# State-space layer and FP4 feed-forward on one core: x kept in place, written-out start lists, 54 unread fp32 products

## What is computed

```python
def _L0_attn_ref(x, A, B, C, D, gamma, beta):
    xB = jnp.einsum('bsh,nh->bsn', x, B)
    xD = jnp.einsum('bsh,oh->bso', x, D)
    def step(state, xb_t):
        state = state @ A.T + xb_t
        return (state, state)
    ...
    out = jnp.einsum('bsn,hn->bsh', states, C) + xD
    ...
    return (out - mu) * rsqrt(var + LN_EPS) * gamma + beta

def _L0_ffn_ref(x, w_gate, w_up, w_down):      # 256 -> 704 -> 256
    gate = fp4_linear(x, w_gate)               # both operands rounded to FP4,
    y = fp4_linear(x, w_up)                    # one scale for 16 elements
    h = jax.nn.silu(gate) * y
    return fp4_linear(h, w_down)

x = _layernorm(x + _L0_attn_ref(x, ...))
x = _layernorm(x + _L0_ffn_ref(x, ...))
```

## Time and profile before

| | us |
|---|---|
| median of 3 runs | 607.63 |
| the profiled run | 608.48 |
| its span | 606.7 |
| outside its span | 1.78 |
| first x load issued | 1.75 |
| first product of tile 0 (`layer`) | 75.86 |
| `gu0` of tile 0 | 96.93 |
| `gu0` of tile 3 | 124.74 |
| span end | 606.7 |

### The profile page before, as it was taken

The page is one execution under the profiler, slowest core; times in us unless marked ns, Lnnn a source line. Parts: engine busy times, 40 slices in busy tenths (PEclk is TensorE's granted clock), DMA queues, the critical chain, the costliest instruction groups (busy, mean ns, idle before and its releaser), DMA issues.

```text
span 606.7 us, 12733 instructions
## 1 busy us (share of the span) xinstructions
PE 566.4 (93%) x3699; PEld 504.2 (83%) x3699; DVE 511.2 (84%) x1226; ACT 473.2 (78%) x1424; POOL 494.2 (81%) x672
## 2 busy tenths in 40 slices
PE   7986577899999999999999999999999999999974
PEld 6763555799999999999999999999999999999864
DVE  4484124699999999999999999999999999999971
ACT  2663255578888888888888888888888888888763
POOL 3243163789999999999999999999999999998642
PEclk9997676899999999999999999999999999999997
DMA  6653031111112111111111111111111111100001
GB/s 214 261 202 102 2 84 39 33 38 39 56 56 58 55 57 57 56 55 55 55 55 55 55 55 55 55 55 55 55 55 55 55 55 55 55 26 18 18 21 41
DMA packets 46268, 38.35 MB, mean 63 GB/s; under 512 B 7008, under 2 KB 44960, under 8 KB 45216
## 3 DMA queue, kind: packets, MB, share of 16 engines
q1 hardware_dynamic: 46240, 38.00, 20.6%
HBM read 19.50 MB, written 8.39 MB: 46 GB/s over the span
## 4 chain that ended last, share of the span: by engine, by line
PE 85%; DVE 6%; ACT 3%; DMA 2%; issue 2%; SPq 1%; POOL 1%; POOLq 0%; DVEq 0%; ACTq 0%
PE gu L1089 39%; PE turned L1089 18%; PE yb L1089 7%; PE turned L1143 7%; DMA scratch<-in_L_attn_x_dram 2%; PE turned L1110 2%; PE yb L978 1%; PE yb L1100 1%; PE gu L978 1%; PE turned L1154 1%; PE turned L1153 1%; PE grid L919 1%; DVE scratch L858 1%; DVE htLo L887 1%; PE gu L1011 1%
## 5 line engine op out<-in xcount | busy, mean ns | idle before, releaser
L1089 PE MATMUL gu<-wguHi,xtHi 128*128 128x512 f32 (+1 forms) x384 | 152.7, 398 | 0.4 <-DVE xtLo L851 0.2
L1089 PE MATMUL gu<-wguLo,xtHi 128*128 128x512 f32 (+1 forms) x384 | 145.2, 378 | 0.0
L1089 PE MATMUL gu<-wguHi,xtLo 128*128 128x512 f32 (+1 forms) x384 | 145.2, 378 | 0.0
L1089 PE MATMUL turned<-wdHi,htHi 128*128 128x256 f32 x320 | 92.3, 289 | 3.8 <-DVE htLo L887 3.8
L499 POOL TENSOR_TENSOR scratch<-scratch 128x704 f32<-128x704 f32 x64 | 92.2, 1441 | 2.5 <-DVE scratch L872 1.8
L1089 PE MATMUL turned<-wdHi,htLo 128*128 128x256 f32 x320 | 91.8, 287 | 0.0
L1089 PE MATMUL turned<-wdLo,htHi 128*128 128x256 f32 x320 | 90.9, 284 | 0.0
L504 POOL TENSOR_TENSOR scratch<-scratch 128x640 f32<-128x640 f32 x64 | 81.9, 1279 | 9.6 <-DVE scratch L882 9.6
L1089 PEld LDWEIGHTS gu<-wguHi,xtLo 128*128 128x128 f32 x384 | 73.1, 190 | 12.6
L1089 PEld LDWEIGHTS gu<-wguHi,xtHi 128*128 128x128 f32 x384 | 73.3, 191 | 10.3 <-DVE xtLo L851 1.0
L1089 PEld LDWEIGHTS gu<-wguLo,xtHi 128*128 128x128 f32 x384 | 73.3, 191 | 8.7
(11 more groups left out here) (191 smaller groups left out, 1650.8 us busy)
## 6 DMA issues: line engine op xcount, KB each, us to landing
scratch<-in_L_attn_x_dram SPq DMA_DIRECT2D x8, 1024.0 KB, 5.0
xtTile<-xT SPq DMA_DIRECT2D x64, 128.0 KB, 2.3
scratch<-in_L_attn_x_dram SPq DMA_DIRECT2D x64, 128.0 KB, 2.4
out_dram<-scratch SPq DMA_DIRECT2D x64, 128.0 KB, 1.9
stTile<-statesHi SPq DMA_DIRECT2D x128, 8.0 KB, 1.8
stTile<-statesLo SPq DMA_DIRECT2D x64, 8.0 KB, 1.7
scratch<-in_L_ffn_w_down_dram SPq DMA_DIRECT2D x1, 704.0 KB, 6.2
scratch<-in_L_ffn_w_up_dram SPq DMA_DIRECT2D x1, 640.0 KB, 6.0
```

Of the source, the lines that this page charges most:

```text
L1089: ins = nc.tensor.matmul(to, l, r, start=(first and q == 0), stop=(last and q == len(passes) - 1))
```

## The change

1. **x in place.** `xRaw` goes. x is loaded into `xT` itself, transposed from there and copied back to the same place (`x_columns`), so no load waits. `xT` is laid out by half, token, and then columns; `load_columns` reads 256 columns of a partition in one piece. The transposes of the second half use `grid` in place of `yb`, and the weights' transposes have two banks in place of three.
2. **Buffers.** The tiles' buffers lie over parts of `scratch` that are used up earlier, or in free room; the output of `mean_square` that nobody reads goes to `yb` and not to `junk`.
3. **Lists.** The preamble and the first six to eight steps of the tiles (VectorE 6, TensorE 7, ScalarE and GpSimd 8) are written out call by call on ScalarE, VectorE, TensorE and GpSimd; the tables are gone. From then on `run` is as before. Two copies of the x groups (0 and 28) go to VectorE. SyncE issues all loads of x and weights without a wait between them, then the small ones.
4. **Silu table.** ScalarE's first instruction is a Silu of one column that nobody reads.
5. **Unread products.** The transposes of `busy` become fp32 products, 10 of them at the start. The 42 others go; in their place `unread_up` adds 54 fp32 products of the identity: 6 before the first `layer`, 24 from there to `gu0` of tile 0, and 4 ahead of each `gu0` of tiles 1 to 6.

The loop, the last steps and all arithmetic that is read are as before. Of the diff:

```diff
-        xTile = view(RING * H).rearrange("p (b k) -> p b k", b=RING)
...
+        xTile = view(FREE, RING * H, RING)
...
             def load_x(h):
-                if h >= 2:
-                    sp.wait_ge(s_xt, 4 * (h - 1))
-                sp.dma_start(xRaw[:, h % 2, :], x_v[h].rearrange("p t d -> p (t d)")).then_inc(s_xload[h % 2], 16)
...
+                sp.dma_start(xT[:, h, :, :, :].rearrange("p t c k -> p (t c k)"),
+                             x_v[h].rearrange("p t d -> p (t d)")).then_inc(s_xload[h], 16)
...
-            load_x(4)
+            for h in range(4, HALVES):
+                load_x(h)
...
-            sp.wait_ge(s_xtc, 4)
+            copied(sp, 3)
             for tile in range(RING):
                 load_columns(0, tile)
+            for tile in range(RING):
+                sp.dma_start(xTile[:, tile, :], x_v[0, :, tile, :]).then_inc(s_ldx[tile], 16)
+            sp.wait_ge(s_sthi, 1)
+            load_states(0, 0, (0, 1))
             sp.wait_ge(s_states, 1)
-            load_states(0, 0)
-            sp.wait_ge(s_xt, 4 * HALVES)
-            sp.wait_ge(s_wlo, len(W_GROUPS))
+            load_states(0, 0, (2,))
...
+            act.wait_ge(s_half, 1)
+            nc.scalar.activation(unread[:, :], neg_half[:, :], ACT.Silu)
...
             def busy(n):
                 for _ in range(n):
-                    nc.tensor.transpose(wbanks[1][:, 0:P], ident[:, :], ident[:, :])
-
-            busy(12)
+                    nc.tensor.matmul(wbanks[1][:, 0:P], ident[:, :], ident[:, :], start=True, stop=True)
+
+            def unread_up(n):
+
+                for _ in range(n):
+                    nc.tensor.matmul(gu[:, 0:P], ident[:, :], ident[:, :], start=True, stop=True)
...
+                    if not isinstance(tile, int) or tile >= 1:
+                        pe.wait_ge([s_silu, s_h, s_hsc][k], done(h, m - 1))
+                        if k == 0 and isinstance(tile, int) and tile <= 6:
+                            unread_up(4)
```

More of the change, by code:

```diff
@@ L264, in ssm_fp4_ffn, with copied, run @@
         PEELED = 2
-        def run(eng, ops, after={}):
+        def copied(eng, u):
+            eng.wait_ge(s_xtc, sum(k not in VECTOR_COPIES for k in range(u + 1)))
+            if min(VECTOR_COPIES) <= u:
+                eng.wait_ge(s_xtcv, sum(k in VECTOR_COPIES for k in range(u + 1)))
+        def run(eng, ops, first):
             last = max(lag for _, lag in ops)
@@ new lines, in _ @@
+            ve1(0, 4)
+            norm2(0, 3)
+            t_hi(0, 6)
+            silu_gate(0, 1)
+            nm2(0, 4)
+            h_abs(0, 0)
+            x_abs(0, 3)
+            sq2(0, 4)
+            ve2(0, 4)
+            states_hi(1)
+            x_hi(0, 2)
+            nr2(0, 4)
+            norm2(0, 4)
+            mean_square(0, 5)
+            t_hi(0, 7)
+            ve1(0, 5)
+            h_hi(0, 0)
+            nm2(0, 5)
+            h_abs(0, 1)
+            silu_gate(0, 2)
+            x_abs(0, 4)
@@ new lines, in _ @@
+            link(0, 1)
+            w_recip(5)
+            link(0, 2)
+            w_lo(2)
+            link(0, 3)
+            w_lo(3)
+            link(0, 4)
+            w_lo(4)
+            link(0, 5)
+            w_lo(5)
+            link(0, 6)
+            w_sum(4)
+            w_sum(5)
+            link(0, 7)
+            w_grid(4)
+            w_grid(5)
+            states_lo(0)
+            xt_copy(28)
+            w_lo(6)
+            w_lo(7)
+            w_lo(8)
+            w_lo(9)
@@ L1095, in layer @@
                 tile = h * CHUNK + m
+                if isinstance(tile, int) and tile == 0:
+                    copied(pe, 15)
+                    pe.wait_ge(s_cstack, 48)
                 pe.wait_ge(s_tlo, done(h, m))
@@ L1155, in ffn_down @@
                                  stop=True).then_inc(s_dn, 1)
-            def fill_links(h, m):
-                tile = h * CHUNK + m
-                if isinstance(tile, int):
-                    if tile == 1:
-                        chunk_states(1)
-                    for k in FILL_CHAIN.get(tile, ()):
-                        link(1, k)
-            gu0, gu1, gu2 = (ffn_up(k) for k in range(3))
-            run(pe, [(h_turn, 6), (gu1, 4), (gu2, 4), (x_turn, 3), (layer, 0), (fill_links, 0), (ffn_down, 6), (gu0, 3)],
-                {0: [lambda: pair_sums(BATCH - 1)]})
+            gu0, gu1, gu2 = (ffn_up(k) for k in range(3))
@@ new lines, in _ @@
+            unread_up(4)
+            layer(0, 1)
+            chunk_states(1)
+            unread_up(4)
+            link(1, 0)
+            layer(0, 2)
+            link(1, 1)
+            unread_up(3)
+            link(1, 2)
+            unread_up(4)
+            link(1, 3)
+            unread_up(4)
+            x_turn(0, 0)
+            unread_up(3)
+            layer(0, 3)
+            gu0(0, 0)
+            link(1, 4)
+            gu1(0, 0)
+            x_turn(0, 1)
+            gu2(0, 0)
@@ new lines, in _ @@
+            link(1, 5)
+            layer(0, 4)
+            gu0(0, 1)
+            link(1, 6)
+            gu1(0, 1)
+            link(1, 7)
+            gu2(0, 1)
+            link(1, 8)
+            x_turn(0, 2)
+            layer(0, 5)
+            gu0(0, 2)
+            h_turn(0, 0)
+            gu1(0, 2)
+            layer(0, 6)
+            gu2(0, 2)
+            x_turn(0, 3)
+            ffn_down(0, 0)
+            gu0(0, 3)
+            run(pe, [(h_turn, 6), (gu1, 4), (gu2, 4), (x_turn, 3), (layer, 0), (ffn_down, 6), (gu0, 3)], FILLED["pe"])
```

712 lines of the change are left out of this document (491 added, 221 removed).

## The result

The changed kernel takes **604.33 us** (median of 11 runs, 603.05 to 606.44) against 607.63 of the kernel before in the same series; the ratio is 0.9947, 95% interval 0.993 to 0.9964. It is faster, by 3.3 us. The forecast was 592.7 with a range of 580 to 602: the direction was right, the size was not, and the time lies outside the range. The profiled run took 604.36 us, its span is 602.6; forecast was a span of 591.8. So 10.8 us have to be found.

A forecast was written before the change was run, and what follows sets the result against it. A long even part bounded by TensorE behind an uneven start; the start of `gu0` of tile 3 decides. Span 606.7 - 17.9 + 3.0 = 591.8, plus 1.8 outside it 593.6, less the profiled run's 0.9: 592.7 us, range 580 to 602.

The forecast's parts named there:

- The fill's own work: First `layer` to `gu0` of tile 3: TensorE's own work at full clock 39.3 us, 40 with uncovered waits.
- Steps (d) to (f): End of pair 1's sums at 44.5 us to first `layer` at 66.8: states, links, x and weight groups, sums of pair 2.
- With a start at about 2 us the columns land at about 31 us: Start: 11.2 MB ahead of tile 0's columns take 28.8 us at 390 GB/s; stall of some 11 us.
- The upper bound of 16: Stall at tile 0's columns: at most 16 us, if SyncE is held and issues twelve small loads late.
- Step (b): After the columns land: TensorE's nine x and weight groups, 8.1 us at half clock, and two powers, 0.5; ends at 41.0.
- step (c): After (b): `pair_sums(1)` taken at half clock, 3.5 us, ending at 44.5.
- 0.7 of uncovered waits: First `layer` to `gu0` of tile 3: TensorE waits only 0.7 us beyond its own 39.3 us of work.
- rival 2: Fill: clock stays down, half-clock TensorE work adds 17.4 us, giving 610.1; chance 0.06.
- (1) No stall: Start: tile 0's columns land by 20 us, ScalarE goes on 11 us earlier, giving 582.7; chance 0.14.
- (3) Half clock up to the first `layer`: Before the first `layer`: 14 groups of (d) and (e) at 0.9 us, 5.3 more, giving 598.0; chance 0.13.
- (4): Even part: a VectorE or GpSimd step longer by 0.3 us lifts 57 steps, giving 598.4; chance 0.04.
- (5): Start: written lists fit better, waits and half clock in (b) and (c) vanish, 6 us less, 586.7; chance 0.15.

The follow-up runs named there:

- e5_x67_last: Changed kernel with x loads of halves 6 and 7, gamma and beta issued behind the small loads and columns of tiles 0 to 3; 597.48 us.
- g1_all_waits: Changed kernel with late column splits, `tMat` loads ahead of the last four x loads, x of tiles 4 to 7 early, all 54 unread products; 577.27 us.
- e1_beta4: Changed kernel with GpSimd's `add_beta` of tile 4 moved behind `pow2` of tile 0, `t_lo` of tile 3 and `pow1` of tile 1; 601.94 us.
- f1_x_early: Changed kernel with x loads of tiles 4 to 7 issued on SyncE before the first states are waited for; 597.65 us.

## Why the prediction was wrong where it was, step by step

**Right.** A stall at the split of the first columns, with every engine behind it (16.89 us at the named instruction). The product at 0.25 us (0.22), the 12 late ones at 3.0 (2.6 to 3.2). The even part: 100.00 of 100 us on TensorE and 7.59 us a step in both. The fill's own work: with the waits mended, 90.21 - 50.15 = 40.1 us from the first `layer` to `gu0` of tile 3, against 40.0 by the sum. Steps (d) to (f): from the end of the sums of pair 1 at 46.4 to 68.61 are 22.2 us, against 22.3, partly by luck: half clock from 51 to 55 us, which the sum didn't have, stands against sums of pair 2 at 1.93 in place of 2.7. Silu's table at nothing.

**Wrong, the size of the stall.** "With a start at about 2 us the columns land at about 31 us" added up the bytes ahead of the columns and let the columns land when these were through. The bytes came out right, 11.2 MB by 32 us. What failed is the term behind them, which the step put at nothing: from 32 us to the cast at 36.73 the small loads, the columns themselves and their neighbours took another 4.7 us, at 221 GB/s. In e5_x67_last, with 8.9 MB ahead (through by about 26.3 us at the rates of that run), it was 4.6. That is, with the one us by which the bytes were late, the +5.7. The upper bound of 16 comes near the 16.89, by another way: it let SyncE be held and issue twelve small loads late. SyncE was held, 7.05 us for four loads, but the columns, issued at 26.74, still had 2 MB ahead of them, and no run shows that the hold cost anything. The Trainium skill, DMA: Bandwidth & Descriptors, section on queues, rings and completion order, says that completion isn't first in, first out; the loads of `tMat`, 2 to 6 KB, took 15.1 to 16.1 us to land here behind the megabytes, so the small ones didn't pass.

**Wrong, the clock after the stall.** Step (b) and step (c) had half clock through the sums of pair 1. It was at 1.00 from about 41 us, three us after TensorE's return; the sums took 1.9 instead of 3.5 and the groups before them 6.5 instead of 8.6. That is -3.7 of the -3.9, and it hid a good part of the first error. The reason given for (b), idleness before it, held for three us only.

**Wrong, and the largest: "0.7 of uncovered waits" in the fill.** "The other engines allow it" was a sum of VectorE's work and a chain of tile 0. It never asked for what GpSimd's next instruction waits, in the new order, nor when SyncE, with sixteen small issues ahead, sends that load. The stretch from the first `layer` to `gu0` of tile 0 took 23.2 us and not 15.7; with the one order on SyncE changed it took 15.5. Half clock from 79 to 89 us is part of the 7.5, rival 2 on a small scale; how large a part isn't shown. The step counted each engine's work and left out SyncE's order from 60 to 80 us.

**The range** reached to 602 for a first `layer` at 71 and a dear product; it had no case for a new wait in the fill, although there, too, written lists had replaced a planner on four engines. A wait of 5 to 8 us there had its like in the row of 4.95 us at 75.86.

**The rivals.** (1) No stall: not what happened, but its price, 10 to 11 us, was near the 12.6 measured once the split moved. (3) Half clock up to the first `layer`: no, only until 41 us and from 52 to 55. (2) In part, above. (4) and (5) no.

**The end.** 1.2 us more lie behind `gu0` of tile 6, in the last steps after the even part, in which the granted clock is lower: 0.66 over the last 23 us against 0.78 before. I didn't test it.

## What to carry to other kernels

A load that no longer waits is not free: list the one queue that issues it, in order, with 0.6 us for each issue, the bytes ahead of each transfer and, for the small one that is waited for, its own time behind them (4.7 us here), and look what the *first needed* small load stands behind and which list waits for it; here these places were worth 18 us and the whole change 3. When hand-written lists replace a planner, read for every engine what the instruction ahead of the critical one waits for, the DMA queue included. The unread products paid back no more than their own length here, and behind tile 3 nothing: put such work only where TensorE idles, and mend the holes before weighing it.

## What the runs showed of the hardware

- SyncE's issue of a load, 0.4 to 0.6 us, was held while megabytes were under way: 7.05 us for four from 9.10, 5.88 for two in e5_x67_last, and 4.07 for the three small `tMat` loads when these stood there (start 9.80, g1_all_waits); they take 1.86 otherwise. In these three it is not the size of the load that is held but its place.
- TensorE's clock rose on transposes. From 37.98 to 41 us it ran three groups of four transposes and two pairs of 16x16 power products of 0.2 us, after 15.64 us of idleness, and was at full clock soon after 41. Stretches of the kernel after:

```profile
38.00:39.00 1.00, 1.00 (x5) 1.00 (x6) 0.00 (x0) 1.00 (x2) 1.00 (x2) 0.50 0.01 5
39.00:40.00 1.00, 1.00 (x9) 0.67 (x7) 0.81 (x1) 0.73 (x3) 1.00 (x1) 0.50 0.00 0
40.00:41.00 1.00, 1.00 (x8) 0.93 (x8) 0.96 (x2) 0.64 (x2) 0.08 (x1) 0.50 0.00 0
41.00:42.00 1.00, 1.00 (x10) 0.90 (x8) 1.00 (x2) 0.71 (x2) 0.04 (x1) 0.92 0.00 0
```

  The Trainium skill, TensorE: Matmul & The Clock Gate, part 4 on PE-mode transpose, says that transposes don't count as busy for the clock. The measurement speaks against it, for these fp32 transposes, beside which only the four small products ran; the prediction had weighed that rule for its rival 3, which didn't occur. Its own row for the rule, 66 to 70 us at 0.50, has products of link 8 beside the transposes, so it doesn't speak of transposes alone.
- The clock also fell without idleness: at 79 us in e1_beta4 and soon after 51 us in the kernel after, each time within about 1.5 us of the end of a first link (14 records of products with 16 rows, 1.90 us). Behind the second such link of f1_x_early and both of g1_all_waits it stays at 1.00. What decides is open; I made no run for it.
